# Causal attention stage of a transformer tower: class values as three bf16 parts, stack loads split by groups of four heads, first half loaded during the projection

## The chip, the cores and the metric

The kernel runs on one core of one Trainium2 chip. The metric is the device time of one execution, in microseconds (us), median of several runs.

## The reference, cut to what matters

The program is a small tower over 8 sequences of 512 tokens plus one class token each, width 256. The change lies in the attention of the first layer, with 16 heads of 16:

```python
q = (x @ wq.T + bq).reshape(b, s, NH, D).transpose(0, 2, 1, 3)
k = (x @ wk.T + bk).reshape(b, s, NH, D).transpose(0, 2, 1, 3)
v = (x @ wv.T + bv).reshape(b, s, NH, D).transpose(0, 2, 1, 3)
scores = jnp.einsum('bhqd,bhkd->bhqk', q, k) / jnp.sqrt(jnp.float32(D))
att = jax.nn.relu(scores) * causal
att = att / (jnp.sum(att, axis=-1, keepdims=True) + 1e-09)
ctx = jnp.einsum('bhqk,bhkd->bhqd', att, v)
```

The class token is the first key of every sequence, so every query also takes a share of the class token's value. All 8 class rows are equal.

## The kernel before, in words

Tokens are kept as 33 tiles of 128 rows (NT = 33): tile 0 holds the 8 class rows, then four tiles (TB = 4) for each of the 8 sequences (B = 8; the code calls a sequence b). The program is a list of passes with a barrier between them; each pass writes one instruction stream for each engine by hand, with waits on semaphores between them, so the order on each engine is the order of the code.

**The projection, `pass_qkv` (L429).** One tile after the other: POOL works out the norm's factor (L406, L408), DVE applies it (L421), PE transposes the tile, projects q, k (L505) and v (L512), and two tiles later computes the scores of the tile's queries against the class key (L523). ACT takes q and k out of PSUM and rounds them to bf16 (L559, L566), DVE and POOL make the second and third bf16 part (L622, L624, L588). ACT keeps the relu of the class scores in fp32 (L572, tile cls_s). SP stores for each tile the parts (L463, into qk_parts), the values (L466, into v_all) and the class weights (L459, into cls_w). `parts`, `v` and `cls_s` have two buffers, so ACT waits for the store of the tile two before (at L566 and L572) and DVE likewise (L630). The middle 28 of the 33 tiles are a loop of two tiles for each turn (`tiles(eng, 5)`).

**The causal attention, `pass_causal` (L680).** For each sequence it goes through four groups g of four heads (HG = 4), and in each group through four steps kt, one for each tile of keys. Head j of the group has PSUM bank j. In a step PE computes the four heads' scores (L743; 512, 384, 256, 128 queries wide in steps 0 to 3); each is a bf16 product whose 96 rows are six pairs of parts of q and k stacked, the tiles qs and ks ("stacks"). ACT (L802) and POOL (L833) weigh heads 0 and 2, DVE (L863) heads 1 and 3, and PE multiplies the weights of the step before with the values (L757, fp32). A bank takes the next step's scores only when ACT or DVE has read it. In step 0 of each group PE also adds the class token's share for all four heads: one fp32 product of cls_w (16 heads by 512) with vbd, a block-diagonal matrix of the class values (L748). PE turns the result of a group (L769) and DVE divides it (L876) in step 2 of the next group.

SP loads the stacks by halves of the heads (`load_half`, L665): for each half 12 transfers of 16 partitions x 8 heads x 512 (every sixth partition of a stack, L671), one of the values (L672) and one of the class weights (L674), 14 in all. It has one buffer for each half. So for the next sequence it waits at each half until PE has done the last values product of that half (s_pv), then issues the half's 14 transfers; PE waits for all 14 before the half's first scores. Before the first sequence SP issues four small loads (L710 to L713), both halves, and five weight loads for the next pass (L168). The matrix vbd is made from v0 by a product (L732) and a DVE operation (L854). Shapes of other transfers that are spoken of below: L463 is 128x12x128, L466 128x272, L459 16x128, L672 128x4x136, and L2191, in the last pass, 8x16x256 (8 neighbouring partitions, 16 rows of 512 bytes in each).

```python
            with sp.Fori(1, B) as b:
                for half in range(2):
                    sp.wait_ge(s_pv, STEPS * (b - 1) + STEPS // 2 * (half + 1))
                    load_half(sp, io, b, half, ...)
```

## Time and profile before

| what | value |
|---|---|
| runs | 2284.18, 2278.9, 2279.78 us; median 2279.78 us |
| the profiled execution's own time | 2278.18 us |
| its span | 2276.4 us |
| busy: PE, DVE, ACT, POOL | 2098.8, 1594.1, 907.1, 737.6 us |
| projection pass | about 187 us to 314.6 us of the span |
| causal pass | 314.6 us to 553.1 us |

Times inside the span count from its start. The profile lists instructions by line, engine and tile; names of tiles carry the pass (causal_qs is the tile qs of the causal pass, keep_early a region that several passes share). SPq is SyncE's queue, on which transfers are issued: its duration is the time that the issue holds SP, not the transfer's own. "Idle before" is an engine's idle time ahead of an instruction, with what ended it. A fp32 matmul shows as two records.

### The profile page before, as it was taken

The numbers are of one execution on the slowest core, as the hardware profiler recorded it, in microseconds if no ns is written. First come the engines' busy times: TensorE is split into PE (matmuls) and PEld (weight loads), VectorE is DVE, ScalarE is ACT, GpSimd is POOL, SyncE is SP. The second block draws the span as 40 slices with busy tenths as digits, with TensorE's granted clock in tenths as the row PEclk, the third lists the DMA queues.
The fourth block names the chain that finished last, engine by engine and source line by source line (L and its number), as shares of the span: only waits on it lengthen the run. The fifth ranks groups of instructions, "written<-read, shape, count | busy, mean of one in ns | idle before, by whom it ended". The sixth has DMA issues, their size and how long they took to land. (4 is left out here: it accounts for less than half of the span.)

```text
span 2276.4 us, 41030 instructions
## 1 busy us (share of the span) xinstructions
PE 2098.8 (92%) x11587; PEld 1337.9 (59%) x11587; DVE 1594.1 (70%) x4366; ACT 907.1 (40%) x2124; POOL 737.6 (32%) x1350
## 2 busy tenths in 40 slices
PE   7998969998999997999988958999999999999998
PEld 6886833333888885666663316888888523333332
DVE  3336846665677776888866856776777788888882
ACT  1114635553221223444433431222222157777777
POOL 3554525554333332333422101111111423333222
PEclk9998979998999999999998968999999779999999
DMA  4323665443000000000001010212214302232210
GB/s 135 114 90 86 152 181 144 138 133 108 1 0 0 0 0 14 1 0 0 0 24 37 9 31 20 48 37 47 46 38 125 89 10 76 81 95 78 76 44 20
DMA packets 215394, 132.43 MB, mean 58 GB/s; under 512 B 116675, under 2 KB 204309, under 8 KB 215317
## 3 DMA queue, kind: packets, MB, share of 16 engines
q1 hardware_dynamic: 215316, 131.50, 21.4%
q8 instruction: 36, 0.59, 0.1%
q14 instruction: 42, 0.34, 0.0%
HBM read 89.81 MB, written 41.25 MB: 58 GB/s over the span
## 5 line engine op out<-in xcount | busy, mean ns | idle before, releaser
L2547 DVE TENSOR_REDUCE attend_mx<-ps 128x1 f32<-128x512 f32 x512 | 320.9, 682 | 40.5 <-PE ps L2241 39.4
L2384 ACT ACTIVATE attend_w<-ps 128x512 f32<-128x512 f32 x512 | 280.6, 596 | 92.5 <-PE ps L2255 90.7
L1854 PE MATMUL ps<-keep_early,moe_zT 128*128 128x256 f32 x1056 | 243.4, 384 | 6.4 <-DVE keep_h L2009 4.4
L1854 PEld LDWEIGHTS ps<-keep_early,moe_zT 128*128 128x128 f32 x1056 | 196.5, 191 | 43.1 <-DVE keep_h L2009 18.6
L2241 PE MATMUL ps<-keep_x,keep_o 96*128 96x512 bf16 x512 | 209.8, 416 | 5.7 <-DVE attend_mx L2547 4.0
L2255 PE MATMUL ps<-keep_o,keep_x 99*128 99x512 bf16 x512 | 191.6, 384 | 2.7 <-ACT attend_w L2384 2.7
L2009 DVE SCALAR_TENSOR_TENSOR keep_h<-ps,moe_g,keep_h 128x256 f32 (+1 forms) x264 | 127.6, 483 | 61.5 <-PE ps L1854 53.2
L863 DVE SCALAR_TENSOR_TENSOR keep_early<-ps,causal_causal 128x512 f32<-128x512 f32 (+3 forms) x256 | 114.0, 486 | 80.2 <-PE ps L743 80.1
L2241 PEld LDWEIGHTS ps<-keep_x,keep_o 96*128 96x128 bf16 x512 | 50.3, 99 | 183.8 <-DVE attend_mx L2547 136.0
L833 POOL TENSOR_TENSOR keep_early<-keep_early,causal_causal 128x128 f32<-128x128 f32 x256 | 113.3, 458 | 128.7 <-ACT keep_early L802 127.7
L802 ACT ACTIVATE keep_early<-ps 128x512 f32<-128x512 f32 (+3 forms) x256 | 98.5, 435 | 126.3 <-PE ps L743 126.0
L2273 PE MATMUL ps<-attend_w,keep_early 128*17 128x512 f32 x1024 | 135.5, 598 | 0.0
L1072 PE MATMUL ps<-mlp_zT,keep_early 128*128 128x128 f32 x1056 | 127.7, 280 | 4.6 <-ACT mlp_zT L1114 4.6
L1072 PEld LDWEIGHTS ps<-mlp_zT,keep_early 128*128 128x128 f32 x1056 | 121.4, 193 | 12.3 <-ACT mlp_zT L1114 8.8
L276 PE MATMUL ps<-tok_W,tok_xin 128*128 128x256 f32 x512 | 122.5, 383 | 0.0
L1081 PE MATMUL ps<-keep_early,mlp_f 128*128 128x256 f32 x528 | 119.3, 379 | 0.0
L1081 PEld LDWEIGHTS ps<-keep_early,mlp_f 128*128 128x128 f32 x528 | 100.2, 190 | 13.6
L276 PEld LDWEIGHTS ps<-tok_W,tok_xin 128*128 128x128 f32 x512 | 96.0, 193 | 12.7 <-issue 0.7
L743 PE MATMUL ps<-causal_qs,causal_ks 96*128 96x256 bf16 (+3 forms) x512 | 93.8, 306 | 10.4 <-DMA causal_cls_w<-cls_w 9.9
L743 PEld LDWEIGHTS ps<-causal_qs,causal_ks 96*128 96x128 bf16 x512 | 37.5, 98 | 111.8 <-issue 57.8
L1274 PE MATMUL ps<-fp_wd,fp_hT 128*128 128x256 f32 x396 | 92.9, 385 | 2.8 <-ACT fp_hT L1306 2.8
L757 PE MATMUL ps<-keep_early,causal_v 128*17 128x512 f32 (+3 forms) x1024 | 95.2, 442 | 0.2 <-POOL keep_early L833 0.2
(332 smaller groups left out, 4064.2 us busy)
## 6 DMA issues: line engine op xcount, KB each, us to landing
tok_xin<-in_xk SPq DMA_DIRECT2D x64, 256.0 KB, 2.7
qk_parts<-qkv_parts SPq DMA_DIRECT2D x33, 384.0 KB, 3.2
qk_parts<-moe_parts SPq DMA_DIRECT2D x33, 384.0 KB, 3.2
causal_qs<-qk_parts SPq DMA_DIRECT2D x96, 128.0 KB, 2.7
causal_ks<-qk_parts SPq DMA_DIRECT2D x96, 128.0 KB, 2.7
keep_o<-qk_parts SPq DMA_DIRECT2D x96, 128.0 KB, 2.8
keep_x<-qk_parts SPq DMA_DIRECT2D x96, 128.0 KB, 2.8
v_all<-qkv_v SPq DMA_DIRECT2D x33, 136.0 KB, 3.1
```

Source lines behind the costliest of these rows:

```text
L276: last = nc.tensor.matmul(ps[:, u, 0:D], xin[:, u, k, :], W[:, k // KD, k % KD, :], start=(k == 0), stop=(k == KT - 1))
L743: nc.tensor.matmul(ps[:, j, kt * P:S], ks[:, half, hh + j, kt * P:(kt + 1) * P], qs[:, half, hh + j, kt * P:S], start=True, stop=True).the ...
L863: nc.vector.scalar_tensor_tensor(w[:, j, kt % 2, 0:S - kt * P], ps[:, j, kt * P:S], 0.0, causal[:, 0:S - kt * P], ALU.max, ALU.mult).then_ ...
L1072: last = nc.tensor.matmul(ps[:, bank, m * P:(m + 1) * P], f1[:, k, f0:f0 + P], zT[:, k * P:(k + 1) * P], start=(k == 0), stop=(k == KD - 1))
L1081: last = nc.tensor.matmul(ps[:, F2, 0:D], f[:, m, :], f2[:, m, :], start=(m == 0), stop=(m == KF - 1))
L1854: last = nc.tensor.matmul(ps[:, E0 + pair % 2, e % 2 * D:(e % 2 + 1) * D], zT[:, u, k * P:(k + 1) * P], we[e][:, k, :], start=(k == 0), st ...
L2009: ins = nc.vector.scalar_tensor_tensor(env.h[:, s, :], ps[:, E0 + pair % 2, e % 2 * D:(e % 2 + 1) * D], g[:, u, 3, e:e + 1], env.h[:, s, : ...
L2241: nc.tensor.matmul(ps[:, MX + i % RING, :], qs[0:R, x.buf(0), h, t * P:(t + 1) * P], ks[0:R, x.buf(0), h, :], start=True, stop=True).then_ ...
L2255: nc.tensor.matmul(ps[:, SC + i % RING, :], ks[:, x.buf(2), HG * g + j, kt * P:(kt + 1) * P], qs[:, x.buf(2), HG * g + j, :], start=True, ...
L2273: last = nc.tensor.matmul(ps[2 * HD * j:2 * HD * j + HD + 1, CTX, :], v[:, buf, kt, (HG * g + j) * (HD + 1):(HG * g + j + 1) * (HD + 1)], ...
L2384: nc.scalar.activation(w[:, j, kt % 2, :], ps[:, SC + (HG * k + j) % RING, :], ACT.Exp)\
L2547: nc.vector.tensor_reduce(mx[:, t, k:k + 1], ps[:, MX + (TB * k + t) % RING, :], AX, ALU.max)\
```

## The change

1. In the projection the class weights are kept as three bf16 parts instead of fp32. ACT writes the relu twice (fp32, and the first part), POOL makes the others (`class_parts`, three operations of 16x128 for each tile), and SP stores them with three transfers for each tile (`class_out`), in six copies so that they form a stack, cls_parts, as q has. The buffers become four, and the store of tile s is issued with tile s + 1.
2. The class value itself is split into three parts once (`class_value`, POOL) and put on a block diagonal through DRAM (`class_value_rows`, six stores at tile 4; `load_constants`, seven loads). The class product in the causal pass becomes one bf16 product of 48 rows; v0's product, vbd and the tiles own and pick go.
3. The stacks are loaded by quarters (groups of four heads): 12 transfers of 16x4x512 for each quarter, each with its own semaphore. SP may issue a quarter as soon as the scores of that group of the sequence before are done (s_sc), no longer only when the half's values products are; values and class weights are still loaded by halves, after s_pv. PE waits for the quarter's stacks before its scores, and for values and class weights before the half's first class product.
4. Half 0 of the first sequence is loaded during the projection: 24 stack transfers behind the stores of tile 27 (NT - LATE), two transfers for values and class weights and seven for constants behind those of tile 28. Its buffers are held from before the projection.
5. The projection's loop over tiles is written out on all engines.
6. The row of class outputs (env.o row 0) is computed at the end of the pass on DVE.

```diff
+            for s, u, n in tiles(sp, NT):
                 sp.wait_ge(s_p2, s + 1)
                 sp.dma_start(io["qk_parts"][:, :, :, s, :]...).then_inc(s_out[u], 16)
                 sp.wait_ge(s_va, s + 1)
                 sp.dma_start(io["v_all"][s], ...).then_inc(s_vout[u], 16)
-                if known(s) >= 1:
-                    class_out(s, u)
+                if known(s) >= 2:
+                    class_out(s - 1, 1 - u)
+                if isinstance(s, int) and s == 4:
+                    class_value_rows()
+                if isinstance(s, int) and s == NT - LATE:
+                    for w in range(2):
+                        sp.wait_ge(s_out[w], 16 * 3)
+                        sp.wait_ge(s_vout[w], 16 * 3)
+                    for w in range(4):
+                        sp.wait_ge(s_cout[w], 48)
+                    ahead.first.load_stacks(sp, io, 0, 0)
+                    ahead.first.load_stacks(sp, io, 0, 1)
+                if isinstance(s, int) and s == NT - LATE + 1:
+                    sp.wait_ge(s_diag, 16 * 6)
+                    ahead.first.load_values(sp, io, 0)
+                    ahead.load_constants(sp, io)
...
             def class_out(s, u):
-                sp.wait_ge(s_cls, s)
+                sp.wait_ge(s_clsp, s)
                 sp.sem_inc(s_took, 1)
-                sp.dma_start(io["cls_w"][:, s - 1, :], cls_s[:, u, :]).then_inc(s_cout[u], 16)
+                for part in range(3):
+                    at, n = PQ.index(part), PQ.count(part)
+                    sp.dma_start(io["cls_parts"][:, at:at + n, s - 1, :],
+                                 cls_p[:, s % 4, part:part + 1, :].to_broadcast([NH, n, P])).then_inc(s_cout[s % 4], 16)
...
+            for s, u, n in tiles(pool, NT):
                 ln.on_pool(pool, s, u)
                 if known(s) >= 3:
                     third(s - 3, 1 - u)
+                if known(s) == 3:
+                    class_value()
+                if known(s) >= 5:
+                    class_parts(s - 4)
+            class_parts(NT - 4)
             for s in range(NT - 3, NT):
                 third(s, s % 2)
+                class_parts(s)
...
+    def load_stacks(self, sp, io, b, quarter):
+        at = quarter * HG
+        for c in range(len(PQ)):
+            for m, dst, part in ((self.n, self.qs, PQ[c]), (2 + self.n, self.ks, PK[c])):
+                src = io["qk_parts"][part, m, at * HD:(at + HG) * HD, bass.ds(1 + TB * b, TB), :]                    .rearrange("(h d) n t -> d h (n t)", d=HD)
+                sp.dma_start(dst[c:HD * len(PQ):len(PQ), at:at + HG, :], src).then_inc(self.s_stacks[quarter], 16)
...
         @block.sync
         def _(sp):
...
+            halves[1].load_stacks(sp, io, 0, 0)
+            halves[1].load_stacks(sp, io, 0, 1)
+            halves[1].load_values(sp, io, 0)
+            sp.dma_start(v0[:, :], io["v_all"][0, 0:B, :]).then_inc(s_w, 16)
             env.ahead["mlp"].start(sp)
             with sp.Fori(1, B) as b:
                 for half in range(2):
-
+                    for quarter in range(2):
+                        g = 2 * half + quarter
+                        sp.wait_ge(s_sc[HG - 1], STEPS * (b - 1) + TB * (g + 1))
+                        halves[half].load_stacks(sp, io, b, quarter)
                     sp.wait_ge(s_pv, STEPS * (b - 1) + STEPS // 2 * (half + 1))
-                    load_half(sp, io, b, half, qs[:, half], ks[:, half], v[:, half], cls_w[:, half, :], s_load[half])
+                    halves[half].load_values(sp, io, b)
...
             def class_value(b, g):
+                if g % 2 == 0:
+                    pe.wait_ge(s_values[g // 2], VALUES * (b + 1))
                 past(pe, s_ctxs, NG * b + g - 1)
-                nc.tensor.matmul(ps[:, 4 + g % 2, :], vbd[:, HG * g:HG * (g + 1), :].rearrange("h a d -> h (a d)"),
-                                 cls_w[:, g // 2, :], start=True, stop=False, skip_group_check=True)
+                at = 2 * HD * HG * (g % 2)
+                nc.tensor.matmul(ps[:, 4 + g % 2, :], vb[:, g // 2, at:at + 2 * HD * HG], halves[g // 2].cls[:, :],
+                                 start=True, stop=False, skip_group_check=True)
```

How this moves instructions on SP, before, at the head of the loop over sequences (ISA rows are address arithmetic, the shape is partitions x heads x elements). L671 stands 12 times for a half, then L672 and L674:

```order
L717 ISA
L671 ISA
L671 DMA causal_qs<-qk_parts 16x8x512
L671 ISA
L671 DMA causal_ks<-qk_parts 16x8x512
L671 DMA causal_qs<-qk_parts 16x8x512
```

The same place in the changed kernel, where one quarter's loads end and the next quarter's begin (first_qs and first_ks are the stacks of half 0):

```order
L753 DMA first_qs<-qk_parts 16x4x512
L753 DMA first_ks<-qk_parts 16x4x512
L822 REGISTER_ALU
L753 ISA
L753 DMA first_qs<-qk_parts 16x4x512
L753 ISA
L753 DMA first_ks<-qk_parts 16x4x512
```

Of these transfers there are now 48 for each sequence where there were 24; each moves 4 heads where it moved 8.

SP in the changed projection, behind the loads at tile 27: the stores of tile 28, the values and constants of the first half, and the stores of tile 29:

```order
L753 DMA first_qs<-qk_parts 16x4x512
L753 DMA first_ks<-qk_parts 16x4x512
L484 DMA qk_parts<-qkv_parts 128x12x128
L487 DMA v_all<-qkv_v 128x272
L469 DMA cls_parts<-qkv_cls_p 16x3x128
L469 DMA cls_parts<-qkv_cls_p 16x2x128
L469 DMA cls_parts<-qkv_cls_p 16x128
L757 DMA first_v<-v_all 128x4x136
L759 DMA first_cls<-cls_parts 48x512
L779 DMA first_causal<-in_causal 128x512
L781 DMA first_vb<-diag_parts 8x2x256 x6
L484 DMA qk_parts<-qkv_parts 128x12x128
```

Where a tile had three issues there are five, and 33 loads (24 and 9) have moved in front of the last tiles' stores.

## Rows read from the trace of the kernel before

**Rows 1.** Time by stretch: busy time of each engine, granted PE clock, DMA share

```profile
core 0: us, PE busy (x) PEld busy (x) DVE busy (x) ACT busy (x) POOL busy (x), PEclk, DMA share, GB/s
203.00:305.00 102.00, 102.00 (x745) 84.26 (x745) 83.75 (x192) 63.59 (x200) 59.12 (x82) 1.00 0.68 153
...
382.00:437.00 55.00, 54.00 (x434) 19.52 (x432) 36.04 (x112) 28.72 (x72) 28.32 (x64) 1.00 0.50 139
```

**Rows 2.** Timeline of all engines, one group of four heads (g = 2 to g = 3, first sequence)

```profile
337.77 1.04 PE L743 MATMUL ps<-causal_qs,causal_ks 96*128 96x512 bf16 x4
...
344.50 1.04 PE L743 MATMUL ps<-causal_qs,causal_ks 96*128 96x512 bf16 x4
...
345.15 1.29 DVE L863 SCALAR_TENSOR_TENSOR keep_early<-ps,causal_causal 128x512 f32<-128x512 f32 x2 [0.68 <-PE ps L743]
345.81 1.12 PE L748 MATMUL ps<-causal_cls_w,causal_vbd 16*128 16x512 f32 x2
346.87 0.82 PE L743 MATMUL ps<-causal_qs,causal_ks 96*128 96x384 bf16 x4
```

**Rows 3.** Timeline of the causal pass's start, SP's queue and PE

```profile
314.57 0.36 SPq L710 DMA_DIRECT2D causal_v<-v_all  x1
316.38 0.77 SPq L671 DMA_DIRECT2D causal_qs<-qk_parts  x1
325.43 0.59 SPq L671 DMA_DIRECT2D causal_qs<-qk_parts  x1
328.00 1.86 PE L743 MATMUL ps<-causal_qs,causal_ks 96*128 96x512 bf16 x4 [8.36 <-DMA causal_cls_w<-cls_w]
...
334.31 0.43 SPq L168 DMA_DIRECT2D keep_early<-in_woT  x1
336.88 1.90 SPq L168 DMA_DIRECT2D keep_early<-in_ff_b  x1
```

**Rows 4.** Timeline of SP's queue, two half loads in the loop over sequences

```profile
346.12 0.63 SPq L671 DMA_DIRECT2D causal_qs<-qk_parts  x1
354.79 0.45 SPq L672 DMA_DIRECT2D causal_v<-v_all  x1
355.44 0.35 SPq L674 DMA_DIRECT2D causal_cls_w<-cls_w  x1
359.74 0.60 SPq L671 DMA_DIRECT2D causal_qs<-qk_parts  x1
374.06 0.64 SPq L671 DMA_DIRECT2D causal_qs<-qk_parts  x1
```

**Rows 5.** Transfers by line: ns that an issue held SP, least/median/most

```profile
L671 SPq DMA_DIRECT2D causal_qs<-qk_parts x96: 579/580/1193, 316.4 to 531.4; - x96
L463 SPq DMA_DIRECT2D qk_parts<-qkv_parts x33: 377/382/405, 194.4 to 309.6; - x33
L672 SPq DMA_DIRECT2D causal_v<-v_all x16: 386/450/592, 324.3 to 533.0; - x16
L2191 SPq DMA_DIRECT2D attend_vb<-diag_parts x6: 264/323/326, 1806.0 to 1807.8; - x6
L459 SPq DMA_DIRECT2D cls_w<-qkv_cls_s x32: 330/492/734, 199.8 to 311.0; - x32
```

**Rows 6.** Timeline of the projection's last tiles, SP's queue (stores of tiles 27 and 32)

```profile
290.87 0.38 SPq L463 DMA_DIRECT2D qk_parts<-qkv_parts  x1
...
311.04 0.73 SPq L459 DMA_DIRECT2D cls_w<-qkv_cls_s  x1
```

**Rows 7.** POOL's line in the projection and its 128x128 product in the causal pass

```profile
L588 POOL TENSOR_TENSOR qkv_parts<-qkv_rest,qkv_parts 128x512 bf16<-128x512 f32 x29 | 33.5, 1157 | 18.3 <-DVE qkv_parts L624 17.7
L833 POOL TENSOR_TENSOR keep_early<-keep_early,causal_causal 128x128 f32<-128x128 f32 x256 | 113.3, 458 | 128.7 <-ACT keep_early L802 127.7
```

**Rows 8.** Timeline of the causal pass's end

```profile
544.14 1.12 PE L748 MATMUL ps<-causal_cls_w,causal_vbd 16*128 16x512 f32 x2
552.50 0.62 DVE L876 TENSOR_TENSOR keep_o<-ps,causal_den 128x64 f32<-128x64 f32 x4
```

More of the change, by code:

```diff
@@ L472, in _ @@
             sp.wait_ge(s_vout[1], 16 * (NT // 2))
-            sp.wait_ge(s_cout[0], 16 * (NT // 2))
-            sp.wait_ge(s_cout[1], 16 * (NT // 2))
+            for w in range(4):
+                sp.wait_ge(s_cout[w], 48 * ((NT - 1) // 4))
         @block.tensor
@@ L525, in class_scores @@
                 last.then_inc(s_c, 1)
-            for s, u, n in tiles(pe, 5):
+            for s, u, n in tiles(pe, NT):
                 transposes(s, u)
@@ L642, in _ @@
             ln.stats(dve, env.x[:, 0, :], 0, 0)
-            for s, u, n in tiles(dve, 5, 2):
+            for s, u, n in tiles(dve, NT - 2, 2):
                 ln.apply(dve, env.x[:, s, :], s, u, s_T)
@@ L662 @@
 PK = (0, 1, 2, 0, 1, 0)
-def load_half(sp, io, b, half, qs, ks, v, cls_w, sem):
-    heads = slice(half * HALF, (half + 1) * HALF)
-    for c in range(len(PQ)):
-        for m, dst, part in ((half, qs, PQ[c]), (2 + half, ks, PK[c])):
-            src = io["qk_parts"][part, m, :, bass.ds(1 + TB * b, TB), :].rearrange("(h d) n t -> d h (n t)", d=HD)
-            sp.dma_start(dst[c:HD * len(PQ):len(PQ), :, :], src).then_inc(sem, 16)
-    sp.dma_start(v, io["v_all"][bass.ds(1 + TB * b, TB), :, heads.start * (HD + 1):heads.stop * (HD + 1)]
-                 .rearrange("n p f -> p n f")).then_inc(sem, 16)
-    sp.dma_start(cls_w, io["cls_w"][:, bass.ds(TB * b, TB), :].rearrange("h n t -> h (n t)")).then_inc(sem, 16)
@@ new lines, with __init__, reserve, load_constants @@
+STACKS, VALUES = 16 * 2 * len(PQ), 16 * 2
+class Causal:
+    def __init__(self, nc):
+        self.area = Area(nc, "first")
+        self.s_stacks, self.s_values = self.area.sems("stacks", NG), self.area.sems("values", 2)
+        self.s_const = self.area.sem("const")
+    def reserve(self):
+        self.first = Half(self.area, 0, self.s_stacks[0:2], self.s_values[0])
+        self.causal = self.area.sb("causal", [P, S])
+        self.vb = self.area.sb("vb", [HALF * len(PQ), 2, HALF * 2 * HD], BF16)
+    def load_constants(self, sp, io):
+        sp.dma_start(self.causal[:, :], io["causal"]).then_inc(self.s_const, 16)
+        for c, part in enumerate(PK):
+            sp.dma_start(self.vb[c:HALF * len(PK):len(PK), :, :],
+                         io["diag_parts"][part, 0, :, 0:HALF * HALF * 2 * HD].rearrange("a (h x) -> h a x", h=HALF))\
+                .then_inc(self.s_const, 16)
@@ L2613, in build @@
         for step in PASSES:
-            step(nc, env, io)
+            if step is pass_qkv:
+                env.causal = Causal(nc)
+                with env.causal.area.ctx:
+                    env.causal.reserve()
+                    pass_qkv(nc, env, io)
+                    pass_causal(nc, env, io)
+            elif step is not pass_causal:
+                step(nc, env, io)
 PASSES = [pass_constants, pass_tokens, pass_qkv, pass_causal, pass_mlp, pass_fp4, pass_ssm_in, pass_scan, pass_moe,
```

132 lines of the change are left out of this document (85 added, 47 removed).

## The prediction

> **What bounds the kernel now.** I read the stretches first: in the projection and in the causal pass PE is busy all the time at full granted clock (102.00 of 102 us, 54.00 of 55 us) while ACT and POOL are half idle and DVE is at 82% and 66% [rows 1]. DMA engines are at 0.50 in the causal pass, so bytes don't bound it. Then the timeline of one group of heads: from one group's first scores to the next group's is 344.50 - 337.77 = 6.73 us, and in it the fp32 class product holds PE for 1.12 us, between DVE's end on step 0 (346.44) and the next scores at 346.87 [rows 2]. Then SP's queue, which no share of busy time shows. In the loop twelve stack loads take 354.79 - 346.12 = 8.67 us to issue (0.72 each), values and class weights 1.0 more; the next half's come at 359.74 and the next sequence's at 374.06 [rows 4]. So SP spends 2 x 9.7 = 19.3 us of each 27.9 us (374.06 - 346.12) on issuing, and is free for 8.6. At the pass's start PE waits until 328.00, 13.4 us after SP's first issue at 314.57, because 4 and 14 issues stand before it [rows 3].
>
> **The price that decides: one issue of a stack load.** The 96 rows of L671 hold SP 579 ns at least and 580 in the median [rows 5]. The changed kernel issues the same kind of transfer (three dimensions, 16 partitions six apart, 1024-byte runs), with 4 heads where there were 8, and needs twice as many. Does an issue of half the size cost half? No row has this form. The rows that are there don't follow size: 128x12x128, with 1536 runs, costs 382 ns, 128x4x136, with 512 runs, 450, and a stack, with 128 runs, 580. The cheapest near form, 8x16x256 (also 128 runs), costs 323 ns [rows 5]. So the ends are 0.32 and 0.58 us, and I take 0.58, the row of the same partitions and strides. The Trainium skill ("DMA: Bandwidth & Descriptors", the table of where the 2 us of a DMA go) gives the sequencer's dispatch as about 50 ns and descriptor generation as "small, variable". The first is ten times below the row here, so the measurement decides; by it 48 issues would be free and the third case below would come. The second agrees with a price that size doesn't set.
>
> **Causal pass.** SP's queue for one sequence was 2 x 9.7 us. Now it is 4 x 8.67 + 2 x 1.0 = 36.7, with 0.5 for the added waits 37.2 us. PE needs less than before: a bf16 product of 512 columns takes 1.04/4 = 0.26 us [rows 2] where the fp32 pair takes 1.12, and the next scores are then held by DVE (end at 346.44 and a semaphore), so I count 0.8 us for each of 32 groups, 27.9 - 3.2 = 24.7 us for a sequence. 37.2 is over 24.7: **SP becomes the bound** and the gain on PE isn't seen. The earlier permission (s_sc in place of s_pv) doesn't help a queue that is never idle. Count from SP's first issue of the pass, T:
> - 24 stacks, values and class weights of half 1 at 9.05/14 = 0.646 us each (316.38 to 325.43) [rows 3]: 16.8; v0 0.5; the five weight loads 336.88 + 1.90 - 334.31 = 4.5 [rows 3]. T + 21.8.
> - Seven sequences at 37.2: T + 282.2.
> - The last load (values of half 1, sequence 7) lands 2.6 us later, as the first half's did (325.43 to 328.00) [rows 3]; only then may PE do the class product of group 2. That group's rest is 6.7 - 0.8 = 5.9, and the last one from its class product to the pass's end 552.50 + 0.62 - 544.14 - 0.8 = 8.2 [rows 8]. T + 298.9.
> - PE stands still before it and starts at a lower clock: the first group of the pass took 337.77 - 328.00 = 9.8 us where the next took 6.7 [rows 2, 3]. I add 3: T + 301.9.
>
> Before, the pass took 553.1 - 314.57 = 238.5 us. **+63.4 us.** The first scores come some 12 us earlier after T, since half 0 and the constants are there, but this isn't seen either: SP's queue starts at T and runs through. The v0, own and pick loads, the product L732 and the DVE operation L854 lie before the first scores, in the same hidden stretch.
>
> **The end of the projection.** The 33 loads put behind tiles 27 and 28 stand in front of the stores of tiles 28 to 32. From the first store of tile 27 (290.87 [rows 6]) SP has: six tiles at 0.38 + 0.60 + three class stores at 0.49 (bounds 0.33 and 0.58) + gaps = 2.75 us, 16.5; one more set of class stores 1.6; 24 stacks at 0.646, 15.5; nine other loads 3.8. Sum 37.4. Behind the last issue lie landing and barrier, 314.57 - 311.77 = 2.8 us [rows 3, 6]. And ACT may write the parts of tile s only when those of tile s - 2 are stored, POOL may make tile 31's third part only behind tile 30's class parts, and these wait for ACT: I add 3.5 for the stretches in which SP then waits for a tile. 43.7 us, where it was 314.57 - 290.87 = 23.7 [rows 3, 6]: **+20 us.** PE has nothing to do meanwhile. The loads gained the start of the next pass, which isn't on the path.
>
> **The rest of the projection.** POOL is busy 59.12 of 102 us for 29 tiles, 2.0 us of the 3.5 us of a tile [rows 1, 7]. It gets three operations of 16x128. POOL's 128x128 product takes 458 ns [rows 7], so they take 1.4 us or less, with four waits of their own. At the upper end POOL needs 3.4 us and more on top of its present waits for DVE (17.7 us of them before L588 alone [rows 7]), and the pace of a tile rises. Bounds 0 and 12 us over 28 tiles, I take **+5**: POOL's waits for DVE leave little. ACT's second relu (some 0.3 us) has room: 63.6 of 102 busy. SP's five issues a tile, 2.75 us, have room at 3.5. The written-out loop saves register work which PE's full row hides; nothing. Class value once: four small POOL operations, in the +5.
>
> **Sum:** 63 + 20 + 5 = +88.5 on the profiled execution's own 2278.2 us: **2367 us**. That execution stands 1.6 us under the median of 2279.8, which I leave, being within 0.1%. Later passes are the same.
>
> **Rivals.**
> 1. *An issue of half size costs 0.45 us*, as the values load does [rows 5]. For: fewer rows for each partition. Against: the three forms above don't follow size. A sequence then takes SP 48 x 0.59 + 2.5 = 30.8 us, still over 24.7. T + 18.4 + 215.6 + 19.7 = T + 253.7, +15; projection end 3 less, +17; +5. 2278 + 37 = 2315 us. Chance 0.14.
> 2. *An issue costs 0.32 us, and SP isn't the bound*: the other side. For: L2191's row, 0.32. Against: it has 8 partitions next to each other, and none in steps of six. SP needs 48 x 0.46 + 2.5 = 24.6 us for a sequence, PE 24.7. Then the class product's 32 x 0.8 = 25.6 us and the start's 328.00 - 314.57 - 1.8 = 11.6 us are gained, and the projection's end costs 20 - 6.3 and its rest 5: -18.5, 2260 us. It decides from about 0.36 us downward. Chance 0.11. The 50 ns that the Trainium skill's page "DMA: Bandwidth & Descriptors" gives for the dispatch would make it this case.
> 3. *No net change*: the price falls between these two. Chance 0.03.
> 4. Within my forecast: POOL bounds the projection (+12 in place of +5), or the class stores cost 0.33: 2360 to 2380; no other sign.
>
> **How the numbers follow.** My case 0.72, spread 2340 to 2390. The range 2300 to 2390 takes in this and most of rival 1, and leaves out rival 2 and the break-even, some 2 in 10. A measurement can tell 0.3%, about 7 us, from no change: faster 0.11 (rival 2), same 0.03, slower 0.86 (mine, rival 1).
>
> **What the profile after would show.** Right: L753's issues at about 580 ns, 384 of them; SP's queue of the causal pass without a gap, 37 us for a sequence; PE waiting for the DMA first_cls or causal_cls before the class product of groups 0 and 2, about 12 us of each 37; PE's share in the pass down from 98% to near 65%, and a granted clock under 1.00 there; the last store of the projection some 20 us later; the causal pass about 300 us. The class product at one record of 0.22 to 0.26 us. Wrong: issues under 0.4 us, a sequence in 25 us, the first scores 2 us into the pass and no waits for stacks after.

## The result, and the profile after

The changed kernel takes 2390.41 us in the median of four runs (2388.59 to 2392.92), the kernel before 2280.76 (four runs, 2278.9 to 2284.18): a ratio of 1.048, 95% interval 1.0462 to 1.0498. The change makes the kernel 110 us slower. The sign and the main mechanism (SP's queue) are those of the forecast; the time lies 23 us above the forecast and 0.4 us outside the range.

The profiled execution took 2390.43 us, its span 2388.6, 112.2 more than before. The page's first part:

```profile
span 2388.6 us, 41184 instructions
PE 2112.2 (88%) x11553; PEld 1344.2 (56%) x11553; DVE 1602.5 (67%) x4364; ACT 914.5 (38%) x2156; POOL 780.4 (33%) x1450
```

Before, PE was busy for 2098.8 us of 2276.4. PE has hardly more to do (13 us, at a lower clock), and the rest of the 112 us is time in which it waits. Busy time by stretch, in the columns of [rows 1], shows where:

```profile
203.00:305.00 102.00, 90.00 (x635) 73.11 (x634) 78.06 (x170) 59.82 (x197) 82.42 (x146) 0.98 0.52 134
358.00:666.00 308.00, 232.80 (x1700) 81.16 (x1700) 148.80 (x455) 117.33 (x288) 113.37 (x256) 0.84 0.38 102
```

The first row is the stretch of the projection in [rows 1]: PE had 102.00 of 102 us and has 90.00, POOL went from 59 to 82. The second is the whole causal pass: PE busy for 76% of it, at a granted clock of 0.84, DMA engines at 0.38. Then SP's queue. The transfers by line (ns that an issue held SP: least, median, most), the counterpart of [rows 5]:

```profile
L753 SPq DMA_DIRECT2D first_qs<-qk_parts x96: 579/580/1537, 312.1 to 625.6; - x96
L753 SPq DMA_DIRECT2D causal_ks<-qk_parts x96: 579/579/964, 359.3 to 644.9; - x96
...
L781 SPq DMA_DIRECT2D first_vb<-diag_parts x6: 654/655/749, 333.4 to 337.0; - x6
```

With qs and ks of both halves these are 384 issues of a stack, and each holds SP for 580 ns, as each of the 192 larger ones did [rows 5]. The timeline of SP's queue, at the values load of half 1, one sequence apart each time, answers to [rows 4]:

```profile
418.11 0.44 SPq L757 DMA_DIRECT2D causal_v<-v_all  x1
...
456.51 0.44 SPq L757 DMA_DIRECT2D causal_v<-v_all  x1
...
494.35 0.44 SPq L757 DMA_DIRECT2D causal_v<-v_all  x1
```

A sequence takes SP 38.4 and 37.8 us, where the period was 27.9 [rows 4]. Before, SP waited 52.6 us for PE in the loop over sequences (the view of SP's waits from 340 us to 540 us: line, what ended the wait, us in total, times, longest):

```profile
SPq L671 <- PE ps L757: 52.6, 14, 7.0
```

The same view of the changed kernel, from 380 us to 650 us, has no wait of SP at all: its queue always has the next issue to do. PE's waits, from 190 us to 700 us (line, what ended the wait, us in total, times, longest):

```profile
PEld ps L853 <- issue: 42.7, 24, 9.4
PE ps L853 <- DMA first_cls<-cls_parts: 36.6, 7, 9.1
PEld ps L853 <- DMA causal_cls<-cls_parts: 35.9, 8, 5.4
PE ps L853 <- DMA causal_cls<-cls_parts: 33.7, 8, 5.1
```

L853 is the class product, now one record (0.39 us for most; 1.12 before, [rows 2]). It's the first instruction of a half that needs the values and class weights, the last things that SP issues for the half. PE and PEld (TensorE's loading of weights) wait at the same places, so their rows aren't to be added.

Last, the projection's end on SP's queue, the counterpart of [rows 6] and of the first row of [rows 3]:

```profile
308.42 0.40 SPq L484 DMA_DIRECT2D qk_parts<-qkv_parts  x1
...
312.10 0.72 SPq L753 DMA_DIRECT2D first_qs<-qk_parts  x1
...
333.35 4.27 SPq L781 DMA_DIRECT2D first_vb<-diag_parts  x6
...
352.72 3.20 SPq L469 DMA_DIRECT2D cls_parts<-qkv_cls_p  x6
358.58 0.66 SPq L753 DMA_DIRECT2D causal_qs<-qk_parts  x1
```

The first row is the store of tile 27 (290.87 before), the last the first issue of the causal pass (T; 314.57 before). The pass's end is taken at the next pass's first load: 553.96 before, 666.18 now. So the 112.2 us fall into three parts:

| part | before | after | more | forecast |
|---|---|---|---|---|
| up to tile 27's store | 290.87 | 308.42 | 17.6 | 5 |
| from there to T | 23.7 | 50.2 | 26.5 | 20 |
| causal pass, from T on | 239.4 | 307.6 | 68.2 | 63 |

### The profile page after: what moved, and what is told of

Its sections match the earlier page's. It is cut to its first block and busy times, and to the rows that moved or that the text cites. A ratio compares the mean times of both kernels' runs of the same rounds, so it can differ in the third digit from the quotient of the medians.

```text
span 2388.6 us, 41184 instructions
## 1 busy us (share of the span) xinstructions
PE 2112.2 (88%) x11553; PEld 1344.2 (56%) x11553; DVE 1602.5 (67%) x4364; ACT 914.5 (38%) x2156; POOL 780.4 (33%) x1450
## 5 line engine op out<-in xcount | busy, mean ns | idle before, releaser
L961 DVE SCALAR_TENSOR_TENSOR keep_early<-ps,first_causal 128x512 f32<-128x512 f32 (+3 forms) x256 | 116.4, 487 | 144.3 <-PE ps L845 142.9
L939 POOL TENSOR_TENSOR keep_early<-keep_early,first_causal 128x128 f32<-128x128 f32 x256 | 113.4, 456 | 196.0 <-ACT keep_early L907 194.9
L2343 PEld LDWEIGHTS ps<-keep_x,keep_o 96*128 96x128 bf16 x512 | 50.2, 99 | 183.4 <-DVE attend_mx L2649 136.0
L407 POOL TENSOR_TENSOR moe_ve<-moe_mv,keep_eps 128x1 f32<-128x1 f32 x33 | 6.6, 200 | 269.9 <-DVE moe_mv L416 269.9
L1360 PE MATMUL ps<-fp_wg,fp_zT 128*128 128x352 f32 x264 | 86.2, 471 | 1.4 <-ACT fp_zT L1434 1.4
L1376 PEld LDWEIGHTS ps<-fp_wd,fp_hT 128*128 128x128 f32 x396 | 76.3, 193 | 18.8 <-ACT fp_hT L1408 3.6
```

Source lines behind the costliest of these rows:

```text
L961: nc.vector.scalar_tensor_tensor(w[:, j, kt % 2, 0:S - kt * P], ps[:, j, kt * P:S], 0.0, causal[:, 0:S - kt * P], ALU.max, ALU.mult).then_ ...
L1376: last = nc.tensor.matmul(ps[:, DN, 0:D], hT[:, k, :], wd[:, k, :], start=(k == 0), stop=(k == KI - 1))
L2343: nc.tensor.matmul(ps[:, MX + i % RING, :], qs[0:R, x.buf(0), h, t * P:(t + 1) * P], ks[0:R, x.buf(0), h, :], start=True, stop=True).then_ ...
```

## The experiments

In this section T is SP's first issue of the causal pass, and "the pass" runs from T to the next pass's first load. Two theories stood at the start. **Mine:** the issue price of 0.58 us does not depend on size, so that twice as many issues make SP the bound; POOL and SP make the projection longer. **The rivals:** quarters aren't the cause, but the new waits, the class parts, the written-out loop or the loads during the projection; or the price has to do with rows or bytes, so that another cut would help.

### The change with its stacks by halves again

```diff
     def load_stacks(self, sp, io, b, quarter):
-        at = quarter * HG
+        if quarter:
+            return
...
-                sp.dma_start(dst[c:HD * len(PQ):len(PQ), at:at + HG, :], src).then_inc(self.s_stacks[quarter], 16)
+                sp.dma_start(dst[c:HD * len(PQ):len(PQ), :, :], src).then_inc(self.s_stacks[0], 16)
```

(and one wait of SP and PE for each half instead of one for each quarter)

> The changed kernel with the stacks loaded by halves again (12 transfers of 16x8x512 for each half; the half's loads wait for the scores of its second group), all else as changed. Theory (the number of issues on SP's queue is the bound): 28 issues for a sequence take SP 2 x 9.7 = 19.4 us, under PE's 24.7 us, so a sequence takes 24.7 to 25.5 us instead of 38.5 and the causal pass about 212 us instead of 306; the projection's end loses 12 issues of 0.65 us, 8 us. Total 2285 to 2292 us, near the kernel before. Rival (the transfers themselves, their landing or the wait for class weights, are slow, whatever their number): the sequence stays above 34 us and the total above 2350.

Measured: 2281.09 against 2278.41 us, ratio 1.0009 (0.9999 to 1.002), a little better than the 2285 to 2292 us expected. Nearly all of the loss is the quarters. T is 350.62, and the pass takes 201.3 us, 38 less than before and 106 less than in the change. Busy time by stretch of this kernel:

```profile
360.00:540.00 180.00, 179.79 (x1588) 67.78 (x1581) 133.68 (x417) 105.79 (x269) 105.64 (x240) 1.00 0.59 166
```

PE is hardly ever idle in it and has the full granted clock. SP waits for PE again (25.0 us in 14 waits from 365 us to 540 us, by the view of waits used above). A sequence takes 24.0 us (24.7 in the prediction's count for PE). Here the gain of the bf16 class product and of the earlier half shows for the first time: -38 us in the pass, against T's +36.

### The kernel before, with quarters alone

```diff
-            src = io["qk_parts"][part, m, :, bass.ds(1 + TB * b, TB), :].rearrange("(h d) n t -> d h (n t)", d=HD)
-            sp.dma_start(dst[c:HD * len(PQ):len(PQ), :, :], src).then_inc(sem, 16)
+            src = io["qk_parts"][part, m, at * HD:(at + HG) * HD, bass.ds(1 + TB * b, TB), :].rearrange("(h d) n t -> d h (n t)", d=HD)
+            sp.dma_start(dst[c:HD * len(PQ):len(PQ), half, at:at + HG, :], src).then_inc(sem, 16)
```

(with a semaphore for each quarter, SP's waits on s_sc and PE's waits as in the change)

> The kernel before with one part of the change alone: stacks by quarters (48 issues for a sequence where there were 24, with the earlier permission s_sc and PE's wait for each group's stacks). Theory: SP's queue takes 38.2 us for a sequence over PE's 27.9, the causal pass takes 325 us instead of 238.5, total 2360 to 2372 us. So most of the slowdown comes from this part alone, even without any of the others. Rival (the split is free, and the loss comes from the projection or the class weights' parts): within 1% of the kernel before.

Measured: 2364.47 against 2278.41, ratio 1.0379 (1.0358 to 1.04). The pass takes 325.2 us, 86 more than before, and its sequences on SP are again 37.8 us apart:

```profile
411.66 0.45 SPq L676 DMA_DIRECT2D causal_v<-v_all  x1
...
449.41 0.45 SPq L676 DMA_DIRECT2D causal_v<-v_all  x1
```

The same period with the fp32 class product as with the bf16 one: SP sets it, and what PE does in between isn't seen. The pass is 17.6 us longer than in the change, which had the first half and the constants loaded before T.

### What sets the price of an issue

64 loads were put into the MLP's pass of the kernel before (L1043), whose results nobody reads, in kinds that differ from the stack load in one or two things each:

```diff
+            run(6, lambda i: (probe[i:96:6, :].rearrange("p (h t) -> p h t", h=8), stack(16, 8, S)))
+            run(6, lambda i: (probe[i:96:6, 0:4 * S].rearrange("p (h t) -> p h t", h=4), stack(16, 4, S)))
...
+            run(6, lambda i: (probe[i:96:6, 0:S], stack(16, 1, S)[:, 0, :]))
+            run(6, lambda i: (probe[16 * i:16 * i + 16, :].rearrange("p (h t) -> p h t", h=8), stack(16, 8, S)))
...
```

> The kernel before with 64 probe loads at the start of the next pass, in which SP's queue is idle for 310 us; they load parts of q into a tile that nothing reads. Six of each form, each form waited for before the next: 16 partitions six apart with 8, 4, 2 and 1 rows of 1024 bytes; 16 neighbouring partitions with 8 rows; 8 partitions twelve apart and 8 neighbouring ones with 8 rows; 16 partitions six apart with 8 rows of 512 bytes; 16 partitions, neighbouring and six apart, with one contiguous row of 8 KB; and 96 partitions with one row of 8 KB each in one transfer. Theory (an issue costs the same whatever it moves): all three-dimensional forms between 0.55 and 0.62 us, two-dimensional ones between 0.33 and 0.60. Rival 1 (the stride of six makes it dear): neighbouring partitions at 0.45 or less. Rival 2 (half as many engines, half the price): the forms of 8 partitions near 0.33. One load of 96 partitions (six times the bytes) costs 0.4 to 0.6 to issue. Total within 1% of the kernel before.

Measured, in a single run: 2279.88 against 2280.8 us; the loads hide. SP's timeline (start, us that the issue held SP), one row for a kind:

```profile
560.07 0.60 SPq L1043 DMA_DIRECT2D mlp_probe<-qk_parts  x1
...
570.88 0.59 SPq L1043 DMA_DIRECT2D mlp_probe<-qk_parts  x1
...
584.03 0.59 SPq L1043 DMA_DIRECT2D mlp_probe<-qk_parts  x1
...
588.27 0.43 SPq L1043 DMA_DIRECT2D mlp_probe<-qk_parts  x1
...
598.17 0.68 SPq L1043 DMA_DIRECT2D mlp_probe<-qk_parts  x1
...
602.38 0.31 SPq L1043 DMA_DIRECT2D mlp_probe<-qk_parts  x1
...
623.88 0.59 SPq L1043 DMA_DIRECT2D mlp_probe<-qk_parts  x1
626.51 0.32 SPq L1043 DMA_DIRECT2D mlp_probe<-qk_parts  x1
```

In this order: 16 partitions six apart with 8, 4 and 1 rows of 1 KB in each: 0.60, 0.59, 0.59. 16 neighbouring partitions with 8 rows: 0.43. 8 partitions twelve apart: 0.68. 8 neighbours: 0.31. 16 six apart with a single row of 8 KB: 0.59. 96 neighbours with a row of 8 KB each, 768 KB in one transfer: 0.32. The three kinds that aren't listed fit: six apart with 2 rows, 0.59; six apart with 8 rows of 512 bytes, 0.60; 16 neighbours with a single row of 8 KB, 0.42. So size sets nothing, from 16 KB to 128 KB, and neither does the number of rows; with the same number of partitions **the distance between them decides** (16: 0.59 against 0.43; 8: 0.68 against 0.31). The number of partitions matters too (16 neighbours 0.43, 8 neighbours 0.31, 96 neighbours 0.32), and these kinds give no rule for it. The rival of 0.45 for half the size falls, and the 0.32 of L2191 [rows 5] goes with its 8 neighbours. The six vb loads of the change (L781) go to 8 partitions six apart and take 0.65 each.

### The change with stack loads to neighbouring partitions

If distance sets the price, another order of the contracted rows should help: q and k only need the same order, so the change is one of an index.

```diff
-                sp.dma_start(dst[c:HD * len(PQ):len(PQ), at:at + HG, :], src).then_inc(self.s_stacks[quarter], 16)
+                sp.dma_start(dst[HD * c:HD * (c + 1), at:at + HG, :], src).then_inc(self.s_stacks[quarter], 16)
```

> The changed kernel with one edit: the six pairs of parts of a stack stand one below the other (partitions 16c to 16c + 15) in place of interleaved (c, c + 6, ...), so a stack load writes 16 neighbouring partitions; the scores sum the same 96 rows in another order. Number and size of loads stay. Theory (number of issues times their price bounds it): the probes gave 0.43 us for neighbouring partitions and 0.59 for six apart, so a sequence takes 38.3 - 48 x 0.16 = 30.6 us on SP, the causal pass 306 - 58 = 248 us, and with 24 issues less dear in the projection's tail the total is 2325 to 2335 us. Rival (such loads land more slowly: in the probes the last of six landed 5.7 us after its issue, and the six moved 768 KB in 8.4 us; a sequence needs 3.1 MB): transfers bound the sequence at 33 to 35 us, total 2345 to 2365.

Measured: 2313.77 against 2280.73, ratio 1.0154 (1.0137 to 1.0172), 77 us faster than the change and better than the 2325 to 2335 us expected. The issues of a stack now take (transfers by line):

```profile
L753 SPq DMA_DIRECT2D first_qs<-qk_parts x96: 316/366/616, 314.1 to 547.3; - x96
```

The transfers, number and size as in the change, go at 366 ns in place of 580, and the pass falls from 307.6 to 230.4 us. That is the most direct test of "SP is the bound", since the number of issues stays and their price falls. A sequence now takes 30.2 and 29.1 us at first and 26.3 to 26.4 later, still more than PE's 24. The stretch and, from the page's part on DMA issues, the transfer's KB and median time from issue to landing:

```profile
400.00:560.00 160.00, 149.55 (x1237) 53.92 (x1240) 105.98 (x326) 84.94 (x212) 83.20 (x188) 0.94 1.05 138
```

```profile
first_qs<-qk_parts SPq DMA_DIRECT2D x96, 64.0 KB, 4.8
```

The DMA share is 1.05, so the DMA engines are full, at 138 GB/s; in the change such a load lands after 2.2 us. Cheap to issue, dear to move. But SP's queue has no wait here either (384 us to 560 us), and one issue follows the other every 0.49 us, so 48 of them are 23.6 of the 26.3 us. SP still sets the pace as far as its queue shows; the DMA engines are at their limit too, and this run doesn't part the two.

### The loads of the first half back at the causal pass's start

```diff
-                    ahead.first.load_stacks(sp, io, 0, 0)
-                    ahead.first.load_stacks(sp, io, 0, 1)
...
+            ahead.load_constants(sp, io)
+            halves[0].load_stacks(sp, io, 0, 0)
+            halves[0].load_stacks(sp, io, 0, 1)
+            halves[0].load_values(sp, io, 0)
             halves[1].load_stacks(sp, io, 0, 0)
```

> The changed kernel with the first half's 24 stack loads, its values and the constants issued at the start of the causal pass instead of behind tiles 27 and 28. Theory: SP's queue bounds the causal pass, so the 33 issues cost the same 21 us there as here; only the stretches go in which SP waited for a tile at the projection's end (6 to 10 us). Projection ends 23 to 28 us earlier, the causal pass takes 18 to 21 us longer, total 2378 to 2388 us. Rival 1 (the loads behind tile 27 stall the projection and nothing pays for it): 2365 or less. Rival 2 (the early start is worth its 12 us): 2395 or more.

Measured: 2394.49 us, ratio 1.052 (1.0497 to 1.0542). T comes 18.4 us earlier (340.16), and the pass is 21.7 longer (329.3). I had expected the move to gain 2 to 12 us; it costs 4, and comes within 1 us of the second rival's 2395. Of the two terms, the pass is near what the theory says (18 to 21 us, the price of 33 issues), and the tail is what it missed: 18.4 us in place of 23 to 28, since SP's waits for tiles didn't go. The prediction took it that the early loads gain nothing, as SP's queue has no gap from T on. This nearly held: where a queue is the bound, moving work along it shifts the time from one part to another. Of the 26.5 us, 19 are these loads (the tail, from tile 27's store to T, is 31.2 us without them); the other 7.5 I put down to the class weights' stores and the waits for tiles, which no run parts further.

The same move in the kernel with stacks by halves:

> e1 with the first half's loads and the constants issued at the start of the causal pass, as e3 did with quarters. SP isn't the bound in the causal pass of e1, so here the early loads are judged alone. Theory: they cost the projection's tail 10 us (e1's pass begins at 350.6, e3's at 340.2) and save the wait for the first scores, 12 to 14 us; total 2 to 5 us above e1. Rival (the early loads' stay in the tail is dearer than what they save): total 3 us or more under e1.

Measured: 2283.02 against 2281.95, ratio 1.0008 (0.9999 to 1.0018). T is 342.30 and the first scores 357.06, 14.8 us behind it, where with early loads they follow T by 0.7. The tail is 31.5 us instead of 42.5, and the pass 216.3 instead of 201.3: in the two profiled executions the early loads gain 4 us, in the medians (2283.02 and 2281.09) 2 us, and against the kernel before, run beside each (ratios 1.0008 and 1.0009), nothing. So even where SP isn't the bound of the pass, loads put in a lump in front of the last tiles' stores gain next to nothing: they hold the stores that the barrier waits for. The comparison also splits the pass's 38 us: 15 are the earlier half (216.3 to 201.3), and the 23 from 239.4 to 216.3 are what 32 class products, each 0.73 us shorter, would give.

### The projection written out, alone

In the kernel before, `tiles(eng, 5)` became `tiles(eng, NT)` on all engines, so that the loop over 28 tiles is written out:

```diff
-            for s, u, n in tiles(pe, 5):
+            for s, u, n in tiles(pe, NT):
```

> The kernel before with the projection's tile loop written out on all engines and nothing else. Theory: PE is busy all the time there, the register work is hidden: within 3 us of the kernel before. Rival (fetching the longer code slows the tiles, and this is part of the 4.05 us that a tile takes in the changed kernel instead of 3.5): 5 to 17 us slower.

Measured: 2281.07 us, ratio 1.0013 (1.0003 to 1.0023); the pace is 3.56 us for a tile, 3.55 before. It costs some 3 us (1.0003 to 1.0023 is 0.7 to 5.2 us), as expected, and nearly none of it up to tile 27's store (291.48, 290.87 before). So the projection's 17.6 us come from elsewhere.

### POOL's class parts left out for three of four tiles

Here the second and third part of the class weights are made only for every fourth tile from tile 6 on; for the others old ones are stored. SP's stores, ACT's relus and all waits for other engines stay; POOL's waits for its own results go with the operations. The base is the kernel with halves.

```diff
             def class_parts(s):
+                if s > 4 and s % 4 != 1:
+                    pool.wait_ge(s_cls, s)
+                    pool.sem_inc(c_cls, 2)
+                    pool.sem_inc(s_clsp, 1)
+                    return
```

> e1 (the changed kernel with stacks by halves) with POOL's three class operations left out for three tiles in four from tile 6 on: the second and third parts of the class weights of those tiles are stale. ACT's second relu, the five stores a tile, the written-out loop and every wait stay. It parts POOL from SP and ACT, which e6 changed together. Theory (POOL's three operations hold the projection): the mean tile falls from 4.05 to 3.5 or 3.6 us, tile 27's store comes at 291 to 297 us instead of 308, and the total is 12 to 16 us under e1's (2265 to 2270). Rival (SP's fifth store or ACT): tile 27's store above 304, total within 4 us of e1.

Measured: 2268.1 against 2281.95 us, ratio 0.9931 (0.9915 to 0.9948), in time as expected (2265 to 2270 us); tile 27's store is at 301.52, which was 308.09 with halves alone. There I had expected 291 to 297. Tiles 12 to 20 take 3.56 us each where they took 4.15, with five issues a tile on SP in both. So in that stretch **POOL, not SP or ACT, sets the tile's pace.** The groups of POOL in the change, from 228 us to 308 us (busy us, mean ns, then idle before them and what ended it):

```profile
L625 POOL TENSOR_TENSOR qkv_parts<-qkv_rest,qkv_parts 128x512 bf16<-128x512 f32 x20 | 23.1, 1153 | 0.0
L409 POOL TENSOR_TENSOR qkv_rs<-qkv_ve,keep_mhalf 128x1 f32<-128x1 f32 x20 | 12.1, 604 | 1.6
L637 POOL TENSOR_TENSOR qkv_cls_p<-qkv_cls_r,qkv_cls_p 16x128 bf16<-16x128 f32 x20 | 10.1, 503 | 3.9 <-POOL qkv_cls_p L635 3.9
L635 POOL CAST qkv_cls_p<-qkv_cls_r 16x128 bf16<-16x128 f32 x19 | 9.8, 516 | 3.2 <-POOL qkv_cls_r L633 3.2
L633 POOL TENSOR_TENSOR qkv_cls_r<-qkv_cls_s,qkv_cls_p 16x128 f32<-16x128 f32 x19 | 8.9, 467 | 0.0
L407 POOL TENSOR_TENSOR qkv_ve<-qkv_mv,keep_eps 128x1 f32<-128x1 f32 x20 | 4.4, 222 | 4.9 <-POOL qkv_cls_p L637 4.9
```

POOL waits for nobody but itself: at L625, where it had waited 17.7 us for DVE [rows 7], the idle time is 0.0. The three class operations are 1.49 us of a tile, and the waits for their own results (3.9 + 3.2 + 4.9 over 20 tiles) 0.6. In its turn DVE waits for POOL's rs of the next tile:

```profile
L422 DVE TENSOR_SCALAR qkv_z<-keep_x,qkv_mv,qkv_rs 128x256 f32<-128x256 f32 x20 | 24.6, 1230 | 12.5 <-POOL qkv_rs L409 12.1
```

### Class parts once for each sequence

The base is again the kernel with halves. The relus of a sequence's four tiles go into one buffer of 512 columns; POOL makes the parts in three operations of 16x512, one in each of the following tiles, so that none waits for the one before it; SP stores them with three issues for four tiles, where it had twelve.

```diff
-                if known(s) >= 2:
-                    class_out(s - 1, 1 - u)
+                if s >= 8 and s % 4 == 0:
+                    class_out((s - 8) // 4)
...
-                if known(s) >= 5:
-                    class_parts(s - 4)
+                if s >= 8 and s % 4 < 3:
+                    class_parts((s - 8) // 4, s % 4)
```

> The changed kernel with stacks by halves (as e1) and the class weights' bf16 parts made and stored once for a sequence (512 columns) instead of once for a tile: three POOL operations and three stores for four tiles, one operation in each of three tiles. Theory (POOL bounds the projection at 4.05 us a tile, by three operations and their waits of 2 us in all): POOL needs 2.0 + 1.2 us a tile, under PE's 3.5, so tile 27's store comes at 291 to 296 us instead of 308; the pass ends some 25 us earlier than in e1, at 320 to 330, and the causal pass takes 201 us as in e1. Total 2245 to 2258 us, under the kernel before. Rival (it is the fifth store on SP, ACT's second relu or the longer code that holds the tiles): tile 27's store stays above 302.

Measured: 2264.51 against 2280.8, ratio 0.9927 (0.991 to 0.9943). Tile 27's store is back at 295.49 and the pace at 3.62, T is 331.22. This is the first version that does all its work and beats the kernel before (the one above leaves parts out), but it misses the 2245 to 2258 us expected: the pass takes 208.0 us instead of 201.3. All of the difference lies at the second sequence; 4 us are a wait for its first half's stacks:

```profile
PE ps L851 <- DMA first_ks<-qk_parts: 3.8, 1, 3.8
```

With halves alone this wait is 0.2 us. These stacks are loaded behind the next pass's weights in both kernels; here the DMA share is 1.12 from 350 us to 360 us, where it was 0.93 at the same distance from T with halves alone. Why it is higher wasn't tested. After the wait the granted clock is low, 0.74 in the mean from 359 us to 372 us, and the values product of 512 columns takes 1.91 us in place of 1.05 (L868): at that clock PE loses some 2.4 us (an estimate: its 9.0 busy us times 0.26), which is most of the rest.

### The early loads spread over tiles 9 to 19

On top of the batched version, the 21 loads of the first half and of the constants are issued two for each tile, from tile 9 on, instead of in a lump behind tiles 27 and 28, and the six stores of the class value one for each tile.

```diff
-                    ahead.first.load_stacks(sp, io, 0, 0)
-                    ahead.first.load_stacks(sp, io, 0, 1)
...
+                if s >= 9:
+                    for load in ahead.loads[2 * (s - 9):2 * (s - 8)]:
+                        load(sp)
```

> e6 with the 21 loads for the first half issued two for each tile behind tiles 9 to 19, and the six stores of the class value one for each tile. Theory: SP has 1.5 to 2 us free in each tile there, so they cost nothing, and the tail from tile 27's store to the next pass shrinks to 23 to 27 us (23.7 before): pass begins at 315 to 322, first scores 1 us later, causal pass 201 us. Total 2238 to 2248 us. Rival (SP or the DMA engines hold the tiles now): tiles slower in the stretch of tiles 9 to 19, total above e6's.

Measured: **2251.51 against 2280.8 us, ratio 0.9868 (0.985 to 0.9885): the fastest version**, 3.5 us above the range expected. T is 319.69, 5 us behind that of before, with a tail of 24.2 us (23.7 before), and the first scores follow T at once:

```profile
319.69 0.65 SPq L762 DMA_DIRECT2D causal_qs<-qk_parts  x1
...
320.43 1.03 PE L868 MATMUL ps<-first_qs,first_ks 96*128 96x512 bf16 x2
```

The pass takes 203.9 us. The pace of tiles 8 to 27 is 3.72 us, where it was 3.62 without the added issues: two more for each tile nearly fit into SP's gaps. They cost 1.9 us over these tiles, as much as the six single stores of the class value gained before (tile 8's store at 224.86 instead of 226.76), so tile 27's store comes at the same time (295.50).

### The same with neighbouring partitions

> e7 (the fastest so far: halves, batched class parts, first loads spread) with the same edit as e8. Theory: SP isn't the bound in e7, so a cheaper issue changes nothing in the causal pass, and little before: within 4 us of e7 (2251). Rival (slow landing of loads to 16 neighbouring partitions): a sequence's 24 loads of 128 KB take 33 us at the probes' rate, over PE's 25, and the total is 2290 to 2320 us.

The edit is the one of the stack load shown above. Measured: 2302.48, ratio 1.009 (1.0077 to 1.0104), 51 us slower than without it: the theory (within 4 us) fell, and the rival (2290 to 2320) held. The stretch of this kernel, and the page's row on its transfers:

```profile
340.00:540.00 200.00, 172.15 (x1346) 61.77 (x1345) 115.53 (x355) 92.67 (x230) 90.04 (x204) 0.88 1.10 129
```

```profile
causal_qs<-qk_parts SPq DMA_DIRECT2D x48, 128.0 KB, 10.0
```

and of the version before it:

```profile
340.00:510.00 170.00, 167.87 (x1466) 62.42 (x1459) 123.84 (x384) 98.36 (x250) 98.01 (x222) 0.99 0.58 155
```

```profile
causal_qs<-qk_parts SPq DMA_DIRECT2D x48, 128.0 KB, 2.7
```

The same bytes: the DMA engines are full (1.10) at 129 GB/s and a load lands after 10.0 us, where they were at 0.58 with 155 GB/s and 2.7 us. Here SP does wait for PE (92.2 us in 11 waits from 340 us to 540 us), so its queue isn't the bound, and PE waits 26.4 us in six waits for the DMA first_ks. So the edit helped where SP was the bound, and harmed where SP wasn't: there the bound is now the landing of the loads.

## Why the prediction was right or wrong

**The price of an issue, 0.58 us: right.** It measured 579 to 580 ns in the median at half the size too, and so rivals 1 and 2 fell. The Trainium skill ("DMA: Bandwidth & Descriptors", "Anatomy of one DMA — SWDGE (gpsimd) path", the table of where the 2 us go) has about 50 ns for the dispatch. That table is for transfers that GpSimd issues, which the prediction didn't say; on SP's queue the stacks' row is over ten times that, and the least of any row shown is 264 ns [rows 5]. For the descriptors the page has "small, variable"; what an issue's price varied with here is the partitions, their distance and number.

**Causal pass, +63.4: right in kind, 68.2 measured**. SP was the bound, with 37.8 and 38.4 us for a sequence where 37.2 was forecast: seven of them took 266.0 us and not 260.4, which makes the 5 us that were missing. SP's first stretch is right to 0.3 us (T + 22.1 where T + 21.8 was forecast), and what follows the last load took some 1.5 us less than its 19.7. PE's waits stand where the prediction put them, at the class product of groups 0 and 2; PE's share was 76% and the clock 0.84. The share was forecast "near 65%". I took PE's work at the full clock: eight sequences of 24.0 us are 192 us, and divided by 0.84 they are 229 us (an estimate), near the 232.8 that PE was busy. The experiment with halves shows the 24.0 us for a sequence that the prediction had as PE's need (24.7), and the one with quarters alone that no other part of the change is needed for the loss.

**"The end of the projection", +20: 26.5 measured.** The step was the right one, three of its terms were too small. "Nine other loads 3.8" is 0.42 for each; they measured 5.75, since six of them, the vb loads, took 0.65 to 0.66. No row had their form: L2191 has the same number of partitions, 0.32, but not the distance [rows 5]. "2.75" for a tile's issues was 3.1 to 3.4: the values' store took about 0.74 and not 0.60, the three class stores 0.6 each in most tiles. "I add 3.5" for waits: 4.2 were at tile 31 alone.

**"The rest of the projection", +5: 17.6 measured, the step that failed.** The bounds were 0 to 12 and the value +5, with "POOL's waits for DVE leave little" for a reason, and the time lies outside even these bounds. POOL's busy time rose to 3.3 us of each tile, and with 0.6 us of waits for its own results in a chain (subtract, round, subtract) it filled 3.9 of the tile's 4.1 us. The prediction sized the three operations rightly (1.4, measured 1.49) and named their waits, but gave these no price, and it took POOL's old waiting time as a reserve, where the runs show POOL as the engine that sets the pace. From tile 8's store to tile 27's, 19 tiles, the pace is 4.08 us where it was 3.55, 10 us. The other 7.5 are there by tile 8, whose store is at 230.95 (223.41 before). Of these, 2.2 are there by tile 1's store (200.46, 198.19 before): POOL makes the class value, in four operations, ahead of that tile's third part (L625):

```profile
197.56 0.69 POOL L652 TENSOR_TENSOR qkv_v0p<-qkv_v0r,qkv_v0p 1x272 bf16<-1x272 f32 x1 [0.18 <-POOL qkv_v0p L650]
...
199.28 1.15 POOL L625 TENSOR_TENSOR qkv_parts<-qkv_rest,qkv_parts 128x512 bf16<-128x512 f32 x1
```

The other 5.3 come from tile 1 to tile 8: 30.5 us for seven tiles, 25.2 before. POOL's longer tiles are in it, and at tile 4 SP issues the six stores of the class value, for which it needn't wait, as the value is ready at 198.3; meanwhile no tile's store goes out:

```profile
215.24 4.87 SPq L478 DMA_DIRECT2D diag_parts<-qkv_v0p  x6
```

With one of these stores for each tile, seven tiles take 24.5 us where the batched version with the six together takes 26.5. So 2 us are the lump, and the rest is the work on the class parts of each tile.

The run with a quarter of POOL's work puts the pace of tiles 12 to 20 on POOL. It brought tile 27's store to 301.52 and not to 295.49, where the batched version had it, which has fewer stores on SP too. Of these 6 us, 3.6 are there by tile 8 (230.40 and 226.76), and up to there POOL had made the parts of the first five tiles as in the change. Which part is SP's wasn't taken apart. From halves alone to the batched version, which differ in the class parts and their stores only, tile 27's store moves by 12.6 us (308.09 to 295.49): so much of the 17.6 is what the parts cost tile by tile, on POOL and SP together.

**Rival 4** ("POOL bounds the projection, +12 in place of +5") names what happened, at too low a price: with it the forecast would have been 2374. The remaining 16 to 17 us are another 5.6 of the projection, 6.5 of the tail and 4.8 of the pass, with its 0.6 to 1.2 us for a sequence. All three terms were too low, so none hid another.

**What the change would have gained:** with quarters undone, the pass gains 38 us (239.4 to 201.3) and the projection gives back 36, 17 in the class parts and the class value, 19 in the tail. The product gained 0.73 us a group (1.12 to 0.39) where the prediction had 0.8 and a record of 0.22 to 0.26. A gain is left where POOL's work is batched (-16 us), and more where the loads are spread as well (-29 us).

## What to carry to other kernels

Price an issue by its own form, its partitions and their distance, and count issues before bytes: a stack load cut in two cost the queue twice, and a queue without gaps made the gains beside it invisible. When an engine gets short dependent operations, count the waits for its own results, and batch until they are few. Loads that are issued early belong where the queue has gaps in every step, not in a lump ahead of the last stores of the stage.

## What the runs showed of the hardware that was not expected

- The time that an issue holds SP follows the partitions, their distance and number, not size: 16 partitions six apart 0.59 us with 16 KB as with 128 KB, 16 neighbours 0.43 (0.366 in the median of a stream), 8 twelve apart 0.68, 8 six apart 0.65, 8 neighbours 0.31, and 96 neighbours with 768 KB 0.32.
- Loads to 16 neighbouring partitions land later: 4.8 us where 64 KB took 2.2, 10.0 where 128 KB took 2.7, with the DMA engines' share at 1.05 and 1.10. In the second case the rate fell, from 155 to 129 GB/s. Which resource is shared there isn't settled by these runs.
- POOL's operations of 16x128 take 0.47 to 0.52 us in the mean, as one of 128x128 does (458 ns, [rows 7]): fewer partitions saved nothing here.
